# A graph layer on one core: only block 0 alone, pairs from block 1 on, b2 spread by TensorE, idle turns, another first order, two finish buffers

## The reference

```python
h = jnp.maximum(_layernorm(x, axis=-1), 0.0)              # x: 6250 x 128
agg = segment_sum(edge_attr, receivers, num_segments=6250) # edge_attr: 106250 x 128
z = jnp.concatenate([agg, h], axis=1)                      # 6250 x 256
out = x + (relu(z @ W1 + b1) @ W2 + b2)                    # W1: 256 x 512, W2: 512 x 128
```

## Time and profile before

| | us |
|---|---|
| median of 3 runs | 212.84 (212.5 to 214.57) |
| profiled execution, its own time | 212.94 |
| its span (first to last instruction) | 211.3 |
| TensorE busy with matmuls | 194.0 (92% of the span) |
| VectorE busy | 132.4 (63%) |
| ScalarE busy | 84.8 (40%) |
| GpSimd busy | 44.7 (21%) |
| moved by DMA | 62.55 MB |

### The profile page before, as it was taken

The page is one execution under the profiler, slowest core; times in us unless marked ns, Lnnn a source line. Parts: engine busy times, 40 slices in busy tenths (PEclk is TensorE's granted clock), DMA queues, the critical chain, the costliest instruction groups (busy, mean ns, idle before and its releaser), DMA issues.

```text
span 211.3 us, 6779 instructions
## 1 busy us (share of the span) xinstructions
PE 194.0 (92%) x2549; PEld 164.9 (78%) x2549; DVE 132.4 (63%) x582; ACT 84.8 (40%) x186; POOL 44.7 (21%) x120
## 2 busy tenths in 40 slices
PE   1698899999999699999999999999999999999990
PEld 1485778778798488798898898887987988978980
DVE  2954863767673966796769577776783874852210
ACT  3323153271632362533713823635337137136120
POOL 5962020222022022201220222022022022200000
PEclk9999999999999999999999999999999999999999
DMA  6899999999999999999999999999999770010100
GB/s 219 262 388 359 377 371 377 376 375 383 390 378 384 376 376 387 376 380 387 354 354 374 323 386 377 319 301 384 304 379 366 248 275 28 5 51 0 50 29 15
DMA packets 44639, 62.55 MB, mean 296 GB/s; under 512 B 1811, under 2 KB 44310, under 8 KB 44604
## 3 DMA queue, kind: packets, MB, share of 16 engines
q1 hardware_dynamic: 44132, 61.66, 82.9%
q10 hardware_dynamic: 472, 0.43, 0.8%
HBM read 58.88 MB, written 3.20 MB: 294 GB/s over the span
## 4 chain that ended last, share of the span: by engine, by line
PE 74%; DMA 11%; DVE 5%; SPq 3%; issue 2%; ACT 1%; DVEq 0%
PE bank L875 20%; PE bank L809 20%; PE bank L846 14%; PE bank L856 13%; DMA xs<-in_x 5%; DMA out_rows<-outrow 5%; PE bank L820 3%; SPq L267 3%; PE bank L830 2%; DMA hidden<-in_dst 1%; DVE aggT L587 1%; SPq L273 1%; PE bank L802 1%; ACT hidden L422 1%; DVE onehot L495 1%
## 5 line engine op out<-in xcount | busy, mean ns | idle before, releaser
L809 PE MATMUL bank<-edges,onehot 128*32 128x128 f32 x1656 | 55.0, 283 | 2.4 <-DVE onehot L495 1.0
L809 PEld LDWEIGHTS bank<-edges,onehot 128*32 128x32 f32 x1656 | 44.9, 113 | 10.1 <-issue 7.1
L875 PE MATMUL bank<-w,hidden 128*128 128x128 f32 (+1 forms) x400 | 48.6, 279 | 0.4 <-DVE outrow L563 0.4
L875 PEld LDWEIGHTS bank<-w,hidden 128*128 128x128 f32 (+1 forms) x400 | 45.8, 189 | 3.3 <-issue 2.4
L422 ACT ACTIVATE hidden<-bank,b_col 128x512 f32<-128x512 f32 (+2 forms) x56 | 34.2, 634 | 35.1 <-PE bank L856 35.1
L587 DVE TENSOR_TENSOR aggT<-bank,aggT 128x32 f32 x277 | 35.6, 190 | 18.9 <-issue 11.0
L391 ACT ACTIVATE xn<-xs,shift,rstd 128x128 f32<-128x128 f32 (+1 forms) x50 | 21.9, 485 | 53.9 <-POOL shift L348 53.8
L341 POOL TENSOR_SCALAR var<-meanvar 128x2 f32<-128x2 f32 (+1 forms) x25 | 7.6, 302 | 132.9 <-DVE meanvar L515 132.9
L495 DVE TENSOR_TENSOR onehot<-relT,iota 128x384 f32<-128x384 f32 x69 | 34.5, 551 | 0.0
L846 PE MATMUL bank<-hT_hi,w_hi 128*128 128x512 f32 (+2 forms) x56 | 22.6, 403 | 0.6 <-DVE hT_lo L531 0.6
L856 PE MATMUL bank<-agg_hi,w_hi 128*128 128x512 f32 (+2 forms) x56 | 21.5, 384 | 0.1
(11 more groups left out here) (94 smaller groups left out, 176.4 us busy)
## 6 DMA issues: line engine op xcount, KB each, us to landing
edges<-in_edge_attr SPq DMA_DIRECT2D x69, 768.0 KB, 9.8
xs<-in_x SPq DMA_DIRECT2D x21, 128.0 KB, 9.3
out_rows<-outrow SPq DMA_DIRECT2D x10, 256.0 KB
w<-in_L_gnn_W SPq DMA_DIRECT2D x3, 256.0 KB, 9.6
out_rows<-outrow SPq DMA_DIRECT2D x4, 128.0 KB, 8.9
xs<-in_x SPq DMA_DIRECT2D x1, 256.0 KB, 7.7
hidden<-in_dst SPq DMA_DIRECT2D x1, 192.0 KB, 3.1
hidden<-in_dst ACTq DMA_DIRECT2D x1, 192.0 KB, 3.2
```

The source lines that it names most:

```text
L809: ins = nc.tensor.matmul(sums_ps[t * W:(t + 1) * W, cols], onehot[:, hots, e, :], edges[:, slot, e * F:(e + 1) * F], start=(g == 0), stop= ...
L875: ins = nc.tensor.matmul(o[0:w, j * F:(j + 1) * F], hidden[:, t, at:at + w], w2[:, t, :], start=(t == 0), stop=(t == HT - 1))
```

## The change

ONES falls from 3 to 1: block 0 is alone, and the pairs begin with blocks 1 and 2 (the pairs 3 and 4, 5 and 6, and so on are the same as before). EARLY falls with it to 1. b2 is loaded as one row of 512 B, TensorE spreads it over the partitions with one matmul against ones, and ScalarE copies it to `b2_all`. A second finish buffer `outrow_2` (in a weight tile that is free by then) takes every other pair. The loads are reordered: the W1 half for the edges goes behind rounds 1 to 3, x runs four blocks ahead instead of three, W2 goes behind round 6, and stores from step 3 on go behind the edge loads of their step. TensorE gets 29 "idle" turns (the identity turned into an unused bank) between its first steps, and TensorE, ScalarE and VectorE have another order in the start and in steps 1 to 3. The core of the diff:

```diff
-    ONES = 3
+    ONES = 1
...
+        b2_row = sums[0:1, 0, 0:F]
+        ones = sums[0:1, 1, 0:P]
+        outrow_2 = w1[:, 1, :].rearrange("p (a n) -> p a n", a=2)
...
-        rel_ps = [hid_ps[0], turn_ps]
+        rel_ps = [hid_ps[2], turn_ps]
         misc_ps = bank[5][:, 384:512]
+        b1_ps = hid_ps[3][:, 0:HT]
+        b2_ps = hid_ps[3][:, P:2 * P]
+
+        def rows_of(s):
+
+            if alone(s):
+                return outrow[:, s % 2:s % 2 + 1, :]
+            return outrow_2 if isinstance(s, int) and (s - ONES) % 2 == 0 else outrow[:, :, :]
...
                 elif len(bs) == 1:
-                    sp.dma_start(out_v[:, s, :], outrow[:, s % 2, :]).then_inc(stored_one[s % 2] if n < NS else stored, 16)
+                    done = stored_one[s % 2] if first_pass else stored
+                    sp.dma_start(out_v[:, s, :], rows[:, 0, :]).then_inc(done, 16)
                 else:
-                    sp.dma_start(out_v[:, bass.ds(bs[0], 2), :], outrow[:, :, :]).then_inc(stored, 16)
+                    done = stored_pair[(s - ONES) % 2] if first_pass else stored
+                    sp.dma_start(out_v[:, bass.ds(bs[0], 2), :], rows).then_inc(done, 16)
...
-            load(1)
+            for r in range(1, 4):
+                load(r)
             load_w1(0)
-            load(2)
-            load(3)
             load(4)
+            load(5)
+            load_x(3)
+            load(6)
             sp.dma_start(w2[:, :, :], W2.rearrange("(t p) f -> p t f", p=P)).then_inc(w2_landed, 16)
-            for r in range(5, RING):
-                load(r)
+            load(7)
             for k in range(NB):
-                if 3 <= k + 3 < NB - 1:
-                    load_x(k + 3)
-                if k + 3 == NB - 1:
+                if k + 4 < NB - 1:
...
-            act.dma_start(b2_all[:, :], b2.partition_broadcast(P)).then_inc(b2_landed, 16)
+            act.dma_start(b2_row, b2.rearrange("(a f) -> a f", a=1)).then_inc(b2_landed, 16)
...
+            round_w1(1)
             normalise(0)
-            round_w1(1)
             h_out(0)
-            round_w1(0)
             normalise(1)
             h_out(1)
+            act.wait_ge(b2_spread, 1)
+            nc.scalar.activation(b1_col[:, :], b1_ps, ACT.Copy).then_inc(b1_ready, 1)
+            nc.scalar.activation(b2_all[:, :], b2_ps, ACT.Copy).then_inc(b2_ready, 1)
             copy_sums(0)
-            act.wait_ge(rel_copied, 5)
-            act.wait_ge(bases_ready, 2)
-            nc.scalar.activation(b1_col[:, :], misc_ps[:, 96:96 + HT], ACT.Copy).then_inc(b1_ready, 1)
+            round_w1(0)
             normalise(2)
             act.wait_ge(b1_ready, 1)
             for k in range(1, NB):
                 early = k <= EARLY
-                if k >= 2:
+                if k >= 3:
                     h_out(k)
                 if not early:
                     copy_sums(k)
                 round_agg(k - 1, chunks_by(k - 1), place(k - 1), group_of(k - 1))
                 if group1(k) is not None:
                     relu(group1(k), group1(k))
+                if k == 1:
+                    h_out(2)
                 if early:
                     copy_sums(k)
                 if k + 2 < NB:
...
-                    if n == ONES:
+                    if n == ONES + 1:
                         dve.wait_ge(stored_one[0], 16 * ((ONES + 1) // 2))
-                        dve.wait_ge(stored_one[1], 16 * (ONES // 2))
-                    if ONES < n < NS:
-                        dve.wait_ge(stored, 16 * (n - ONES))
+                    if ONES + 2 <= n < NS:
+                        dve.wait_ge(stored_pair[(n - ONES) % 2], 16 * ((n - ONES) // 2))
...
             build(0)
+            relative(1, dstB, colB, relB)
             build(1)
-            relative(1, dstB, colB, relB)
-            turned_ab(0, rel_copied, 4 * TILES, P)
-            relative(2, dstC, colC, relC)
-            relative(3, dstD, colD, relD)
+            stats(1)
             rest_of_w1(1)
             rest_of_h(0)
             dve.wait_ge(bases_turned, 1)
             nc.vector.tensor_scalar(base_tab[:, 0:P], row_ps[0:1, 0:P], 0.0, float(N - 1), ALU.max,
                                     ALU.min).then_inc(bases_ready, 1)
-            for r in ROUNDS[0][2:]:
-                build(r)
-            stats(1)
-            rest_of_w1(0)
+            build(2)
+            build(3)
+            turned_ab(0, rel_copied, 4 * TILES, P)
+            relative(2, dstC, colC, relC)
+            relative(3, dstD, colD, relD)
+            rest_of_h(1)
             dve.wait_ge(rel_turned, 2)
             turned_ab(1, rel_copied)
-            dve.wait_ge(rel_turned, 3)
-            dve.wait_ge(bases_turned, 2)
-            turned_cd(rel_copied)
-            nc.vector.tensor_scalar(base_tab[:, P:FULL], row_ps[0:1, P:FULL], 0.0, float(N - 1), ALU.max,
-                                    ALU.min).then_inc(bases_ready, 1)
-            nc.vector.tensor_scalar(base_tab[:, FULL:FULL + 1], colD[:, 0:1], 0.0, float(N - 1), ALU.max,
-                                    ALU.min).then_inc(bases_ready, 1)
             stats(2)
-            dve.wait_ge(rel_copied, 5)
-            build(ROUNDS[1][0])
-            rest_of_h(1)
-            dve.wait_ge(bases_ready, 3)
+            dve.wait_ge(rel_copied, 2)
+            build(4)
+            dve.wait_ge(bases_ready, 1)
             bases = load_bases(0)
             for k in range(1, NB):
                 if k == 1:
                     dve.wait_ge(agg_cleared, CLEARS)
                 add_sums(k - 1, bases)
-                if k >= 2:
+                if k == 1:
+                    rest_of_w1(0)
+                if k >= 3:
                     rest_of_h(k)
+                rest_of_agg(k - 1, k - 1, place(k - 1))
+                if k == 2:
+                    finish(group2(k), group2(k))
                 if k == 1:
-                    for r in ROUNDS[1][1:]:
-                        build(r)
-                rest_of_agg(k - 1, k - 1, place(k - 1))
-                if k + 1 < NB:
+                    build(5)
+                    build(6)
+                    dve.wait_ge(rel_turned, 3)
+                    dve.wait_ge(bases_turned, 2)
+                    turned_cd(rel_copied)
+                    nc.vector.tensor_scalar(base_tab[:, P:FULL], row_ps[0:1, P:FULL], 0.0, float(N - 1), ALU.max,
+                                            ALU.min).then_inc(bases_ready, 1)
+                    nc.vector.tensor_scalar(base_tab[:, FULL:FULL + 1], colD[:, 0:1], 0.0, float(N - 1), ALU.max,
+                                            ALU.min).then_inc(bases_ready, 1)
+                    dve.wait_ge(rel_copied, 5)
+                    build(7)
+                    build(8)
+                    build(9)
+                if 2 <= k < NB - 1:
                     for r in ROUNDS[k + 1]:
                         build(r)
                 if k + 2 < NB:
...
                     dve.wait_ge(over_read, 1)
                     link(nc.vector.tensor_reduce(colD[:, 6:7], over[:, :], AX_X, ALU.max))
                     nc.vector.tensor_scalar(flag[:, :], colD[:, 6:7], 0.0, None, ALU.is_gt).then_inc(flag_ready, 1)
+                if k == 1:
+                    rest_of_h(2)
+                    dve.wait_ge(bases_ready, 3)
                 bases = load_bases(k)
-                if group2(k) is not None:
+                if k > 2 and group2(k) is not None:
...
-                if isinstance(n, int) and n == 2:
-                    pe.wait_ge(hidden_ready, HT)
-                elif not isinstance(n, int) or n > 2:
+                if not isinstance(n, int) or n >= 1:
...
+            def idle(n, to):
+                for _ in range(n):
+                    nc.tensor.transpose(to[:, 0:P], ident[:, :], ident[:, :])
+
             pe.wait_ge(ident_ready, 1)
+            idle(10, hid_ps[3])
             pe.wait_ge(rel_ready, 1)
             turn_ab(0, relA).then_inc(rel_turned, 1)
             turn_column_a(0).then_inc(bases_turned, 1)
+            idle(3, hid_ps[3])
             sum_rounds(0, 0, 1)
-            turn_x(0)
             pe.wait_ge(rel_ready, 2)
             turn_ab(1, relB).then_inc(rel_turned, 1)
-            pe.wait_ge(rel_copied, 2)
+            idle(2, hid_ps[3])
+            turn_x(0)
+            idle(8, hid_ps[3])
+            sum_rounds(0, 1, 2)
             pe.wait_ge(w1_ready, 1)
             layer1_h(0, 0)
-            sum_rounds(0, 1, 2)
-            pe.wait_ge(rel_ready, 4)
+            turn_x(1)
+            sum_rounds(0, 2, 3)
             pe.wait_ge(b1_landed, 16)
             pe.wait_ge(bases_ready, 1)
-            nc.tensor.transpose(misc_ps[:, 96:96 + HT], b1_row[:, :], ident[0:HT, 0:HT])
+            nc.tensor.transpose(b1_ps, b1_row[:, :], ident[0:HT, 0:HT])
+            pe.wait_ge(b2_landed, 16)
+            pe.wait_ge(ones_ready, 1)
+            nc.tensor.matmul(b2_ps, ones, b2_row, start=True, stop=True).then_inc(b2_spread, 1)
```

(83 more changed lines are left out.)

9 lines of the change are left out of this document (5 added, 4 removed).

## The result

The changed kernel takes 210.06 us (median of 20 runs, 209.56 to 212.46) against 212.80 us (20 runs): ratio 0.9899, 95% interval 0.9871 to 0.9926. A second series gave 209.82 against 212.36: 0.9905 (0.9876 to 0.9934). It is 1.0% faster, and its own times are spread over 1.4%.

A forecast was written before the change was run, and what follows sets the result against it. TensorE's entry into the regular part, its work from there and remaining interruptions bound the kernel: 212.94 + 0.9 for the later mark - 1.7 for the wait gives 212.1, as median 212.0; range 209.8 to 213.7.

The forecast's parts named there:

- the first rival: b2's reads made the DMA hole at 7 to 9 us; without them landings come 1.4 us earlier: 210.6, chance 0.30.
- The main line's own range: Whole kernel: forecast of 212.0 us with 211.1 to 212.9 around it, chance 0.50.
- round 9 starts: TensorE takes up round 9 as its edges land, at 32.0 us; TensorE's own path gives the same time.
- from there to `layer1_agg(1, 1)`: From round 9 to layer 1 over the sums of blocks 1 and 2, forecast to start at 41.0 us.
- from there to the mark: TensorE from the first pair's `layer1_agg` through rounds 13 to 17 and layer 2: 11.0 us.
- mark: First `layer1_h` after round 17, entry into the part regular in both kernels; forecast 52.0 against 51.09, 0.9 us later.
- wait at 69 us: TensorE's wait for sums queued on VectorE behind an earlier store; two finish buffers remove it, worth 1.7 us in full.
- b2's price: Gain from removing b2's 128 start reads if they made the DMA hole: 0 to 1.4 us, taken as 0.
- The cost of the new order: From round 9 to the pair of blocks 1 and 2 the new order costs, putting the mark 0.9 us later.
- The chain over split, finish, builds and statistics: ScalarE and VectorE work from round 9's end at 32.9 to the low part of block 2's sums: 8.0 us, 41.0.
- a second condition: Round 12 landed at 38.6 and summed by 39.5, met before ScalarE reaches the copy of block 2's sums.
- The slow rival: Clock rises no earlier, the start without slack up to round 9 becomes the bound: 1.3 us later, 213.3, chance 0.15.

The follow-up runs named there:

- experiment 5: Kernel before the change with one edit: pairs written to two finish buffers in turn, the finish waiting for the store two groups back; 210.84 us, 0.9922.
- experiment 2: Changed kernel with b2 again read 128 times by DMA at the start, no spreading by TensorE and ScalarE; 211.54 us, 0.9956.
- experiment 3: Kernel before the change with b2's 128 reads issued by SyncE behind round 5 instead of by ScalarE at the start; 211.48 us, 0.9956.
- experiment 7: Changed kernel with ScalarE's split of the sums ahead of the copy of the next sums in steps 2 and 3; 208.96 us, 0.9843.
- Experiment 9: Kernel before the change, old order kept, with b2's read behind round 5, two finish buffers and 15 idle turns ahead of round 1; 208.70 us, 0.9825.
- experiment 10: Changed kernel with split ahead of copy, round 5 built and summed earlier and block 1's scale made earlier; 208.14 us, 0.9787.
- experiment 11: The kernel of experiment 10 (split first, real work in the waits) without any idle turn; 208.15 us, 0.9811.
- experiment 1: Changed kernel without any of its 29 idle turns; 214.47 us, 1.0039.
- experiment 4: Changed kernel with one finish buffer again, every pair waiting for the store of the group before; 215.32 us, 1.0121.
- experiment 6: Changed kernel with more idle turns: 30 instead of 6 in step 1 and 16 new ones in step 3; 210.87 us, 0.9945.
- experiment 8: Kernel before the change with 15 idle turns in the three waits ahead of round 1; 211.97 us, 0.9976.
- experiment 12: Changed kernel as it is, run again for another profile and more times; 209.82 us (12 runs).

## Why the prediction was right, and what in it was wrong

The range (209.8 to 213.7) and the sign held; 212.0 was 1.9 too high. The range held because it was wide enough to take in the first rival. The main line's own range, 211.1 to 212.9, missed the result, the result lies in the class that had a chance of 0.26 (below 210.7), and the prediction's own sign of being wrong, more DMA in the first 30 us, came true. The steps against the execution whose clock stayed up:

| step | forecast | measured |
|---|---|---|
| round 9 starts | 32.0 | 30.46 |
| from there to `layer1_agg(1, 1)` | 9.0 us | 8.9 us |
| from there to the mark | 11.0 us | 11.0 us |
| mark | 52.0 | 50.37 |
| wait at 69 us | 1.7 us | 2.2 us in the profile, 1.7 in the medians (experiment 5) |

**The step that failed is b2's price.** "Ends: 0 and 1.4 us; I take 0" should have been 1.4: b2's reads made the hole (experiments 2 and 3), round 9 landed at 19.8 + 10.6 = 30.4 instead of 31.8, and the mark came 1.6 us before the forecast. This was the first rival, at a chance of 0.30, and its 210.6 is near the result. The argument against it, that other transfers are thin in the hole as well, was no evidence: b2's reads are issued by ScalarE and the edges by SyncE, and with the reads in place the rate of all transfers together is 133 GB/s where it is 398 without (experiment 2).

**The cost of the new order was right.** The chain over split, finish, builds and statistics was summed to within 0.1 us (its 8.0 us from 32.9 end at 40.9, where the prediction has 41.0), and with the split taken ahead of the copy `layer1_agg` came 1.7 us closer to round 9 (experiment 7). Part of the match is luck, as a second condition ended at nearly the same time: round 12 waited 0.8 us for its edges and ended at 37.9, and ScalarE took up its copy at 38.01. Experiment 9 shows the cost in the whole kernel: the order with the pair (1, 2), as it was written, takes 1.4 us more than the old one with the same three other parts. It is not a cost of the pair as such, since experiments 10 and 11 keep the pair and are the fastest.

**The size of the wait** was 0.5 us short in the profile of experiment 5, where the delay of a late add reaches TensorE twice in a step, at `turn_sums` and at `layer1_agg`; its medians gained the 1.7 that were forecast. The mark's 1.6 and these 0.5 are 2.1 us, against the 1.9 that the forecast was too high.

**The slow rival** had the right mechanism, a start without slack that the low clock makes the bound, and in experiment 1 it came true. It cost more than the 1.3 us forecast (3 to 4), as the clock not only rose late but was low again in rounds 4 and 5. With the idle turns it didn't decide: before round 0 TensorE had run nothing but turns, and round 0 took 1.01 us at 6.70 with the idle ones, 1.51 us at 6.78 without. The Trainium skill (TensorE: Matmul & The Clock Gate, the part on the PE-mode transpose) says that a transpose doesn't count as activity for the clock gate. These rows contradict that for the turns used here; they list them as MATMUL and don't show whether they ran in the mode that the page speaks of.

**Not foreseen** were falls of the clock behind waits: the prediction takes it to stay up once it has risen. The waits before a fall were 2.34 and 1.75 us in the changed kernel, 3.28 in experiment 4, and only 0.81 in experiments 1, 2, 10 and 11. In the changed kernel the falls cost up to 2.6 us of the mark (52.95 against 50.37), in about 13 of 32 executions by their mean clock; two of the 32 have a profile.

## What to carry to other kernels

When the data rate drops for a moment at the start, move the suspect transfer before pricing it at nothing; one that reads the same row for every partition is a first suspect. A change with several parts can be faster as a whole while its largest part, as written, is a loss: try the small parts on the old order. Idle turns that raise the clock were worth 3 to 4 us where the order had no slack, 0.6 in the old order and nothing once real work filled the same waits, which gained 0.8 us more (experiment 10 against 7).

## What the runs showed of the hardware

- 128 reads of one 512 B row, issued beside the first loads, cut the DMA from 398 and 391 GB/s to 99 and 136 in two successive us (133 and 186 in the changed kernel). Issued behind round 5 they left no hole at 7 to 9 us. Why they do it was not tried.
- Turns alone raise TensorE's clock, but not in every execution: round 0 took 0.86 to 1.01 us in eight of the nine profiles with idle turns (the changed kernel's two and experiments 2, 4, 6, 7, 8 and 9) and 1.51 in the ninth (experiment 10). Without them it took 1.50 or 1.51 in all five (the kernel before and experiments 1, 3, 5 and 11), and the clock was up at 12.9 us at the earliest (experiment 5) and near 20 us at the latest (the kernel before).
- The clock can fall behind a wait of only 0.81 us, with TensorE busy for 4.19 of the 5 us around it (15 to 20 us, clock 0.81 in experiment 10). Behind the same wait and with the same busy time it stayed at 1.00 in experiment 12. Eight of the 14 profiles have at least one fall. In what executions it falls stays open.
